# A graph layer pair on one core: the output stage of 15 of 20 node blocks inside the attention laps

## The reference, cut to what matters

```python
xn = _layernorm(x, ln1_g, ln1_b)
scores = einsum('ehd,ehd->eh', q[dst], k[src] + ep[:, None, :]) * scale * ew[:, None]
m = segment_max(scores, dst); ex = exp(scores - m[dst]); s = segment_sum(ex, dst)
attn_out = segment_sum((ex / s[dst])[:, :, None] * v[src], dst).reshape(n, D) @ Wo + bo
x = x + alpha * attn_out
xn = _layernorm(x, ln2_g, ln2_b)
x = x + beta * (gelu(xn @ W1 + b1) @ W2 + b2)        # FF = 1024
out = _layernorm(x1 + x)
```

## Time and profile before

| | |
|---|---|
| median of 3 runs | 2775.41 us |
| the profiled execution, time | 2778.12 us |
| its span | 2776.4 us |
| attend (first edge gather to last sum stored) | 1458.7 to 2568.1 us |
| output | 2568.7 to 2776.4 us |
| busy over the span | PE 74%, DVE (VectorE) 80%, ACT (ScalarE) 54%, POOL (GpSimd) 59% |

### The profile page before, as it was taken

One profiled execution on the slowest core, in us unless ns is written; L12 is line 12 of the kernel. 1 busy time (PEld: TensorE's weight loads), 2 busy tenths in 40 slices (PEclk: granted clock), 3 DMA queues, 4 the chain that ended last, 5 costly groups with the idle time before them and its releaser, 6 DMA issues. The chain is left out here.

```text
span 2776.4 us, 40815 instructions
## 1 busy us (share of the span) xinstructions
PE 2060.2 (74%) x9125; PEld 1546.8 (56%) x9126; DVE 2219.0 (80%) x3394; ACT 1511.1 (54%) x4899; POOL 1641.5 (59%) x1849
## 2 busy tenths in 40 slices
PE   1599999999999999939942555555555555555898
PEld 0477777778777787713312444444444444444776
DVE  6488888888888888855545888888888888888555
ACT  0587788788788788713313443434343434343666
POOL 4366666666666666532226777777777777775011
PEclk8799999999999999959976777777777777777999
DMA  2522222222222232258958777777777777775000
GB/s 97 169 83 84 82 82 84 81 84 84 82 84 82 82 84 83 78 100 250 256 158 237 202 202 201 201 202 202 202 202 200 201 203 201 202 202 146 10 13 15
DMA packets 157716, 382.66 MB, mean 138 GB/s; under 512 B 47715, under 2 KB 62435, under 8 KB 157443
## 3 DMA queue, kind: packets, MB, share of 16 engines
q0 software_dynamic: 101968, 313.67, 40.5%
q1 hardware_dynamic: 55458, 57.41, 7.6%
q10 hardware_dynamic: 272, 11.42, 1.2%
HBM read 356.99 MB, written 36.80 MB: 142 GB/s over the span
## 5 line engine op out<-in xcount | busy, mean ns | idle before, releaser
L1503 PE MATMUL ps_sum<-kv_e,ident 128*128 128x264 f32 x1536 | 565.3, 545 | 513.5 <-DVE kv_e L1558 513.5
L1396 POOL DMA_INDIRECT kv_e<-kv_rows,edge x768 | 726.7, 946 | 240.9 <-issue 231.2
L449 ACT ACTIVATE vsh<-feat,rec_a 128x256 f32<-128x256 f32 x1980 | 806.5, 495 | 21.7 <-DMA feat<-in_x_rows,idx 21.7
L417 POOL DMA_INDIRECT feat<-in_x_rows,idx x668 | 673.9, 1009 | 237.7 <-issue 236.2
L1503 PEld LDWEIGHTS ps_sum<-kv_e,ident 128*128 128x128 f32 x1536 | 420.0, 280 | 658.7 <-DVE kv_e L1558 553.3
L496 PE MATMUL ps_a<-msg,hot 128*128 128x257 f32 x1312 | 408.8, 393 | 0.0
L498 PE MATMUL ps_a<-msg,hot 128*128 128x256 f32 x1312 | 390.6, 379 | 0.0
L1525 DVE TENSOR_TENSOR kv_e<-kv_e,ps_query 128x2048 f32<-128x2048 f32 x96 | 219.7, 2288 | 129.7 <-DMA kv_e<-kv_rows,edge 129.7
L500 PE MATMUL ps_a<-msg,hot 128*128 128x192 f32 x1312 | 320.0, 325 | 0.0
L1455 ACT ACTIVATE ps_exp<-score 128x64 f32<-128x64 f32 x96 | 21.9, 228 | 539.5 <-DVE score L1548 539.5
L498 PEld LDWEIGHTS ps_a<-msg,hot 128*128 128x128 f32 x1312 | 248.6, 190 | 36.1
(11 more groups left out here) (344 smaller groups left out, 2937.0 us busy)
## 6 DMA issues: line engine op xcount, KB each, us to landing
ef<-in_ef_t SPq DMA_DIRECT2D x84, 256.0 KB, 4.5
kv_e<-kv_rows,edge POOLq DMA_INDIRECT x768, 3.7
rows_e<-in_ef_t ACTq DMA_DIRECT2D x1, 11152.0 KB, 42.6
rows_e<-rows SPq DMA_DIRECT2D x41, 272.0 KB, 3.4
feat<-in_x_rows,idx POOLq DMA_INDIRECT x668, 2.8
kv_rows<-kv SPq DMA_DIRECT2D x20, 260.0 KB, 2.5
xw<-in_x_rows SPq DMA_DIRECT2D x22, 128.0 KB, 2.7
emb<-in_emb_t SPq DMA_DIRECT2D x166, 16.0 KB
```

Of the source, the lines that this page charges most:

```text
L417: pool.indirect_dma_start(out=feat[:, u, c, 0, :, :].rearrange("p a b -> p (a b)"), out_offset=None, in_=g.x_rows, in_offset=bass.Indirect ...
L449: ins = act.activation(vsh[:, u % TURN, c, j, :, :], feat[:, u % TURN, c, 0, :, :], ACT.Copy, scale=rec_a[:, u % 2, c, 1 + j:2 + j])
L1396: pool.indirect_dma_start(out=kv[:, u, s, :], out_offset=None, in_=g.kv_rows, in_offset=bass.IndirectOffsetOnAxis(ap=edge[:, u, s, DH + 1: ...
L1503: mm = pe.matmul(out, g.ident[:], kv[:, u, s, D:], start=(s == 0), stop=False, skip_group_check=True)
```

## The change

1. Output work in the laps. `stage_ready` also builds a table `lap_window`: the window that is done by each lap (or NOBODY, a spare row). In the 23 laps of the loop every engine has one piece of output work behind each step. VectorE: `divide` behind step 0, `spread` (statistics of the first norm) behind 2, `norms` behind 3. ScalarE: `normed_out` behind 0, `attention_out` with 4 gelus behind 1, `deviations` with 4 gelus and a square root behind 2. TensorE: `turn_attention` with half of the hidden layer, `project` with the other half, `outputs`, `turn_normed`. Each lap does the pieces of three windows in different phases; the pieces run in all 23 laps, whether a window is done or not. SyncE loads one window of `x1` for each lap, and POOL scatters one window's result (`put`) behind its step 3. Sums that VectorE made (bias, `x1`) are now products with the identity on TensorE.
2. `stage_output` has 5 windows left (LEFT = 20 - LAPPED), written out without a loop and without the unused 21st; it loads their `x1` itself and its scatters no longer wait for one another.
3. `kept` is one VectorE operation of 264 elements behind `values`, in place of the 8 on ScalarE, which waits for it before `keep`.
4. The exponentials go to a part of `ps_query`, whose next query is copied one step ahead (LEAD = 3), which frees PSUM for the pieces.
5. Ranks are reversed, so that windows with few edges come first. The weights are loaded by SyncE in `stage_ready`, between `q` and `dst_c`; alpha and beta are multiplied into the weights by VectorE at the start of attend.

```diff
@@ stage_order @@
             then(dve.tensor_reduce(rank_f[:], hit[:], AX.X, ALU.add))
+            then(dve.tensor_scalar(rank_f[:], rank_f[:], -1.0, float(NODES_PAD - 1), ALU.mult, ALU.add))
@@ stage_project @@
+            sp.dma_start(g.x1_rows[NODES_PAD:, :], g.x_rows[NODES_PAD:, :]).then_inc(p_w, 16)
@@ stage_ready, SyncE: ten loads between q and dst_c @@
+            sp.dma_start(g.w_o[:], g.Wo.rearrange("(k p) n -> p k n", p=P)).then_inc(d_q, 16)
+            sp.dma_start(g.w_1[:], g.W1.rearrange("(k p) n -> p k n", p=P)).then_inc(d_q, 16)
+            sp.dma_start(g.w_2[:], g.W2.rearrange("(k p) n -> p k n", p=P)).then_inc(d_q, 16)
...
@@ stage_ready, VectorE @@
+            then(dve.tensor_scalar(late[:], g.node[0:WINDOWS, 0:1], 4.0, None, ALU.mult))
+            then(dve.tensor_tensor(late[:], late[:], after[:], ALU.max))
+            then(dve.tensor_scalar(late[:], late[:], 2.5, None, ALU.add))
...
+                dve.wait_ge(d_win, b * 2 + 2)
+                dve.tensor_scalar(g.lap_window[:, bass.ds(b * 128 + 2, 128)], ps_s[0:1, 128:256], float(NOBODY), None,
+                                  ALU.add).then_inc(d_link, 1)
@@ stage_attend, SyncE @@
+            with sp.Fori(0, whole) as t:
+                out = done_window(sp, t + 2)
+                sp.wait_ge(w_pe, t * 4 + 4)
+                sp.dma_start(x1[:], g.x1_rows[bass.ds(out * P, P), :]).then_inc(w_x1, 16)
@@ stage_attend, POOL, behind step 3 @@
+                pool.wait_ge(w_dve, t * 3 + 3)
+                pool.sem_inc(v_asked_pool, 1)
+                pool.indirect_dma_start(
+                    out=g.out, out_offset=bass.IndirectOffsetOnAxis(ap=to[:], axis=0),
+                    in_=res[:], in_offset=None).then_inc(w_put, 16)
@@ stage_attend, ScalarE @@
-                act.wait_ge(v_fade, k + 1)
-                for h in range(HEADS):
-                    at_h = slice(h * HEAD, (h + 1) * HEAD)
-                    ins = act.activation(kept[:, u % BANKS, at_h], ps_o[:, (u - 1) % BANKS, at_h], ACT.Copy,
-                                         scale=fade[:, u, h:h + 1])
-                ins.then_inc(v_kept, 1)
-                query(u, w)
+                query((u + LEAD) % RING, before)
                 if ahead:
                     part((u + 2) % RING, (t + (u + 2) // RING) * 16 + 16)
+                act.wait_ge(v_kept, k + 1)
+                act.sem_inc(v_asked_act, 1)
                 keep(k, u - 1)
...
+            def normed_out(t):
+                act.wait_ge(w_pe, t * 4 + 4)
+                act.activation(y[:], ps_f[:, 0:D], ACT.Copy)
+                for n in range(2):
+                    act.activation(xn_t[:, n, :], ps_a[:, n * P:(n + 1) * P], ACT.Identity,
+                                   bias=g.ln2_shift[:, n:n + 1], scale=g.ln2_gain[:, n:n + 1])
+                act.activation(both[:], ps_a[:, D:], ACT.Copy).then_inc(w_act, 1)
+            def attention_out(t):
+                act.wait_ge(w_pe, t * 4 + 5)
+                act.activation(att_t[:].rearrange("p a b -> p (a b)"), ps_a[:, 0:D], ACT.Copy)
+                for f in range(HALF):
+                    ins = gelu(f)
+                ins.then_inc(w_act, 1)
+            def deviations(t):
+                act.wait_ge(w_pe, t * 4 + 6)
+                for f in range(HALF, FT):
+                    gelu(f)
+                act.wait_ge(w_dve, t * 3 + 5)
+                act.activation(dev[:], mv[:, :, 1], ACT.Sqrt, bias=eps[:]).then_inc(w_act, 1)
@@ stage_attend, TensorE: the pieces behind steps 0 to 3 @@
+            def turn_attention(t):
+                pe.wait_ge(w_act, t * 3 + 1)
+                hidden(range(HALF))
+                pe.wait_ge(w_dve, t * 3 + 4)
+                for n in range(2):
+                    mm = pe.transpose(ps_a[:, n * P:(n + 1) * P], att[:, n * P:(n + 1) * P], g.ident[:])
+                mm.then_inc(w_pe, 1)
+            def project(t):
+                pe.wait_ge(w_act, t * 3 + 2)
+                hidden(range(HALF, FT))
+                for n in range(2):
+                    pe.matmul(ps_a[:, D:], att_t[:, n, :], g.w_o[:, n, :], start=(n == 0), stop=False,
+                              skip_group_check=True)
+                pe.matmul(ps_a[:, D:], g.ident[:], g.b_o[:], start=False, stop=False, skip_group_check=True)
+                pe.wait_ge(w_x1, t * 16 + 16)
+                pe.matmul(ps_a[:, D:], g.ident[:], x1[:], start=False, stop=True,
+                          skip_group_check=True).then_inc(w_pe, 1)
+            def outputs(t):        # b_2, both, then 8 products of gel with w_2
+                pe.wait_ge(w_act, t * 3 + 3)
+                output(t).then_inc(w_pe, 1)
+            def turn_normed(t):
+                pe.wait_ge(w_dve, t * 3 + 6)
+                pe.matmul(ps_a[:, D:], g.ident[:], x1[:], start=False, stop=True, skip_group_check=True)
+                for n in range(2):
+                    mm = pe.transpose(ps_a[:, n * P:(n + 1) * P], xn[:, n * P:(n + 1) * P], g.ident[:])
+                mm.then_inc(w_pe, 1)
@@ stage_attend, VectorE @@
+                dve.wait_ge(v_fade, k + 1)
+                dve.wait_ge(v_sum, k + 1)
+                dve.tensor_tensor(by_head(kept[:, u % BANKS, :]), by_head(ps_o[:, (u - 1) % BANKS, 0:HEADS * HEAD]),
+                                  fade[:, u, :].rearrange("p (h d) -> p h d", d=1).broadcast_to([P, HEADS, HEAD]),
+                                  ALU.mult).then_inc(v_kept, 1)
+            def spread(t):
+                dve.wait_ge(w_pe, t * 4 + 6)
+                dve.bn_stats(stats[:, 0, :], ps_a[:, D:]).then_inc(w_link, 1)
...
+            def norms(t):
+                out = done_window(dve, t)
+                dve.wait_ge(w_act, t * 3 + 3)
+                dve.reciprocal(rstd[:], dev[:]).then_inc(w_link, 1)
+                dve.wait_ge(w_link, t * LINKS + 4)
+                dve.tensor_scalar(xn[:], ps_a[:, D:], mv[:, 0, 0:1], rstd[:, 0:1], ALU.subtract, ALU.mult)
+                dve.wait_ge(w_put, t * 16 + 16)
+                dve.tensor_scalar(res[:], y[:], mv[:, 1, 0:1], rstd[:, 1:2], ALU.subtract, ALU.mult)
+                dve.tensor_copy(to[:], g.ids[:, bass.ds(out, 1)])
+                dve.wait_ge(w_pe, t * 4 + 7)
+                dve.bn_stats(stats[:, 1, :], ps_f[:, 0:D]).then_inc(w_link, 1)
...
```

More of the change, by code:

```diff
@@ L38 @@
 FF = 4 * D
+FT = FF // 128
 EPS = 1e-5
@@ L1400, in _ @@
+            for u in range(RING):
+                step(whole, u)
+            pool.wait_ge(w_put, whole * 16)
             pool.wait_ge(v_edge[0], laps * 16 + 16)
@@ new lines, in _, with step @@
+            pe.sem_inc(w_pe, 4)
+            def step(k, u):
+                pe.wait_ge(v_acc, k + 1)
+                pe.wait_ge(v_fade, k + 1)
+                out = ps_o[:, u % BANKS, 0:HEADS * HEAD]
+                for half in range(2):
+                    pe.wait_ge(v_msg, k * 2 + half + 1)
+                    for s in range(half * HALF, (half + 1) * HALF):
+                        mm = pe.matmul(out, g.ident[:], kv[:, u, s, D:], start=(s == 0), stop=False,
+                                       skip_group_check=True)
+                    mm.then_inc(v_used, 1)
+                pe.wait_ge(v_kept, k + 1)
+                pe.matmul(out, g.ident[:], kept[:, u % BANKS, :], start=False, stop=True,
+                          skip_group_check=True).then_inc(v_sum, 1)
@@ new lines, in output @@
+            def output(t):
+                pe.matmul(ps_f[:, 0:D], g.ident[:], g.b_2[:], start=True, stop=False, skip_group_check=True)
+                pe.matmul(ps_f[:, 0:D], g.ident[:], both[:], start=False, stop=False, skip_group_check=True)
+                for f in range(FT):
+                    mm = pe.matmul(ps_f[:, 0:D], gel[:, f, :], g.w_2[:, f, :], start=False, stop=(f == FT - 1),
+                                   skip_group_check=True)
+                return mm
+            def outputs(t):
+                pe.wait_ge(w_act, t * 3 + 3)
+                output(t).then_inc(w_pe, 1)
@@ new lines, in turn_normed @@
+            def turn_normed(t):
+                pe.wait_ge(w_dve, t * 3 + 6)
+                pe.matmul(ps_a[:, D:], g.ident[:], x1[:], start=False, stop=True, skip_group_check=True)
+                for n in range(2):
+                    mm = pe.transpose(ps_a[:, n * P:(n + 1) * P], xn[:, n * P:(n + 1) * P], g.ident[:])
+                mm.then_inc(w_pe, 1)
+            pe.wait_ge(v_const, 16)
+            with pe.Fori(0, whole) as t:
+                for u, piece in enumerate((turn_attention, project, outputs, turn_normed)):
+                    step(t * RING + u, u)
+                    piece(t)
@@ L1510, in _ @@
+            for u in range(RING):
+                step(whole * RING + u, u)
         @block.vector
@@ L1561, in _ @@
             keys(0, 0, 0)
             with dve.Fori(0, whole) as t:
-                for u in range(RING):
+                for u, piece in enumerate((divide, None, spread, norms)):
                     k = t * RING + u
@@ L1717, in _ @@
```

(6 more changed lines are left out.)

354 lines of the change are left out of this document (220 added, 134 removed).

## The result

The changed kernel takes 2658.94 us (median of 4 runs, 2658.13 to 2660.74), against 2775.56 us for the kernel before on the same chip (4 runs, 2774.46 to 2776.86): a ratio of 0.958, with a 95% interval of 0.956 to 0.960. It is 116.6 us faster; 108.6 were forecast. The profiled execution's span is 2656.4 us, that of before 2776.4.

What follows compares the result with a forecast made beforehand. POOL was taken to bound attend, VectorE 10% behind. Terms -142.3 - 1 + 0.3 + 35.4 + 2.5 - 4.0 + 0.5 = -108.6 us, off the median 2775.4, gave 2667 us; range 2655 to 2708.

Steps and rivals of the forecast that it cites:

- POOL bounds the laps: In attend, POOL waits for nobody and sets the lap: 45.06 us before, 46.35 with one added scatter.
- The laps' term: In attend's 23 laps, the lap grows from 45.06 to 46.6 us: +35.4 us.
- POOL's bare bound: In the laps, only POOL's added scatter of 1.29 us a lap counts: +29.7 us in 23 laps.
- The output stage: Fifteen windows of 9.48 us leave it, -142.3 us; unused half behind the last window -1; `x1` load +0.3.
- ScalarE's order: In the laps, ScalarE's added work leaves each exponential just in time, costing 0 to 0.4 us a lap.
- third rival: In the laps, each ScalarE table switch costs 1.38 us more: lap 53.0 us, time 2813; chance 0.03.
- second rival: In the laps, TensorE stays at the low clock and becomes the bound: 55.6 us a lap, 2873; chance 0.04.
- first rival: In `norms`, VectorE waits for TensorE's `outputs`: 2706 us with half the bursts low, 2745 with all; chance 0.37.
- Ready: In `stage_ready`, small VectorE operations add about 1.5 us and ten loads ahead of `dst_c` 1: +2.5 us.
- Start of attend: At attend's start, weight loads no longer crowd the first gathers: first `kv_e` gather after 4.2 us, not 8.2; -4.0 us.
- Order and project: The extra copy in project and the reversed ranks cost +0.5 us, with still 96 steps.

Runs made afterwards that it cites:

- both experiments: Rescaling (`kept`) put back on ScalarE in the changed kernel: 2657.68 us, ratio 0.9589; rescaling alone moved to VectorE in the kernel before: 2771.71 us, ratio 1.000.
- the last experiment: Ten weight loads issued behind `dst_c`, against the changed kernel with LAPPED = 17: 2634.42 us, where that kernel without the move took 2637.40.

## Why the prediction was right, point by point

1. **POOL bounds the laps**: right. 46.35 us a lap forecast for POOL, 46.34 by its rows and 46.31 by the steps (the last four have no scatter); taking away its scatter gave 20.5 us.
2. **The laps' term was mis-sized.** The step that failed: "I take 46.6, near POOL's number because most of a read is covered, and above it because two engines so close do not overlap perfectly". They do overlap: +29.6 us measured against +35.4, and POOL's bare bound was +29.7. Two things in it were wrong. VectorE's lap was not 45.9 to 47.7 us but 45.4. The register reads, priced at up to 0.89 us each, cost nothing that shows: no idle time stands before L1756 and L1777, the operations behind them. (The 6.4 / 21 = 0.30 us a lap before L1716 stand where the loop turns.) And the added operations follow each other with less than their durations: `kept` costs 0.33 us a step and not 0.44, which alone is 0.4 us a lap, and L1781 begins 0.46 us after L1779, which takes 0.54. The second: VectorE was 2% short of the bound, and that cost nothing here. The ring of four buffers between the two engines may be why; no run changed it.
3. **The output stage**: 15 x 9.48 was right as a sum, -143.0 forecast, -146.0 measured. Of the missing 3 us, 1.7 are the windows that stayed: their four periods, left as they were in the forecast, take 36.2 us in place of 37.9, because a window written out takes 9.25 us, as the kernel with `LAPPED = 0` shows, and the last one less. The other 1.3 us lie in the stage's start and end and were not told apart.
4. **`kept`**: 0.44 forecast, 0.426 measured as its duration (0.33 in the chain, point 2), its waits never met. That it costs nothing was an outcome of point 1 and is shown by both experiments.
5. **ScalarE's order**: forecast just in time, 0 to 0.4 us late. It had some 1.4 us in hand behind step 2, and behind step 1, where 0.2 were forecast, 0.9 (the exponential at 1790.78, 0.23 us long, and L1742 at 1791.90). The root behind the gelus of step 2 ended 10.1 us after VectorE's last operation before the exponential, where I had 10.4, so the count was right up to there; the tail to the exponential was shorter, and VectorE, behind POOL, asked later.
6. **Table changes**: 1.28 us each and no more, as in the earlier trace rows. The third rival fell. The 1283 ns of the Trainium skill ("ScalarE: Activation LUTs", What ACT_TABLE_LOAD costs) agree; its drain of about 1380 ns shows behind none of the loads here (the pause before L1491 stands ahead of its load).
7. **TensorE**: the clock rose from 0.77 to 0.84, "above 0.8" as forecast, and VectorE never waited for `ps_ff`. First and second rival didn't come. The bounds for `outputs`, 5.2 to 10.4 us, hold: 6.1 (1753.65 to 1759.77) at 0.74, with 1.5 us to spare. At 10.4 it would have been late by 2.8, so the first rival was not far off.
8. **Ready**: +2.5 forecast, +2.9 measured (ready's start to the first edge gather, 33.66 against 30.80 us). The loads' share was taken at 1 us and is 2.7, by the last experiment. The rest, taken at 1.5, is then 0.2. The sum came out close because the two errors cancel.
9. **Start of attend**: -4.0 forecast for the crowd that is gone, -3.5 measured.
10. **Order and project**: the +0.5 can't be seen. From the last reduction of the ranks (L721, L718 before) to the start of ready it is 227.0 us in the changed kernel's trace and 225.5 in that of the kernel before, but it varies between 223.2 and 227.6 over the profiles of all kernels.

The laps (5.8 us less than forecast), the output stage (3.0 less), ready (0.4 more) and the start (0.5 more) add up to 7.9 of the 8.0 us between the forecast and the result.

The spans differ by 120.0, the medians by 116.6: ready began 3.0 us earlier in this execution (1424.89 against 1427.93), because the message stage, which the change leaves alone, was ahead by 4.6 (its last gather starts at 1169.2 against 1173.8). The other profiled executions start ready between 1421.4 and 1427.5.

## What to carry to other kernels

Count the instructions that the busiest issuer gets, here one scatter in a lap, and price a move of work by these alone; what lands on the other engines was free here up to their slack, which the idle time before their first operation of a step gives directly (add what the engine's chain grows by, not the operations' durations). When a tail stage is moved into a loop, its gain is (pieces moved) x (time of each), so look first for how many more pieces the loop can still take. Large loads that nobody wants soon belong behind the small urgent ones on a queue: here that starts the sort 2.7 us earlier.

## What was not expected of the hardware

In the timeline of the start, the first edge gather took POOL 1.69 us, where the 84 of the laps took 79.4 / 84 = 0.945 on average. Beside it VectorE ran L1700, a tensor_scalar over 2048 elements of each partition, from SBUF to SBUF, 1458.84 to 1460.12; POOL's gather ended at 1460.24, 0.12 us behind it. The kernel before has no such operation there, and its first edge gather took 0.97 us. All profiles of the changed kernel and its variants show 1.68 or 1.69. The Trainium skill ("SBUF — State Buffer", A bandwidth-pool intuition that's wrong (but worth ruling out)) has GpSimd kept from writing its descriptors while VectorE holds the port that they share, until some 115 ns after VectorE's end; the trace agrees in the time. No run moved L1700 away, so that the port is the cause is not shown here. It happens once and costs 0.7 us.

The other surprise is the chip whose attend stage takes 20% longer in the same kernel, 1321.6 us against 1099.8, with its other stages unchanged. A ratio of 0.9735 there and 0.9581 elsewhere describe the same two kernels.
